# An eleven-stage kernel on one core: head projections in f32, expert chunks of 1024 tokens, and splits a batch ahead

## The reference

```python
h = _L0_tok_ref(x, ...)                       # ((gamma * (q @ k.T)) @ v) @ Wo + bo, PReLU
h = concatenate([h, txt], axis=1)
h = h + _L0_attn_ref(_layernorm(h), ...)      # 8 heads of 8, relative bias, softmax; out @ proj_w + proj_b
h = h + _L0_ffn_ref(_layernorm(h), ...)       # 16 experts, top 2, relu
h = h + _L1_attn_ref(_layernorm(h), ...)      # linear attention, D_inv = 1/max(q.k_sum, 1e-6); out @ Wproj.T + bproj
h = h + _L1_ffn_ref(_layernorm(h), ...)       # causal attention with 4 heads of 16, x + y @ wo.T, then 8 experts with
                                              # hidden 170, top 2, silu(x @ w1.T) * (x @ w3.T) @ w2.T
```

## Time and profile before

| | us |
|---|---|
| median of three runs | 2953.19 (2952.58 to 2969.43) |
| the profiled execution | 2956.11, its span 2954.3 |
| TensorE busy | 2502.1 (85%), granted clock 0.897 of full |
| VectorE, ScalarE, GpSimd busy | 2019.2, 1629.4, 400.4 |
| `mix`, from the span's start | 0 to 284 |
| `prj` | 1347 to 1415 |
| `lpr` | 1912 to 1974 |
| `cpj` | 2482 to 2569 |
| second expert stage | 2569 to the end |

### The profile page before, as it was taken

How to read it: one execution, slowest core, us unless ns; L and a number is a source line. 1 busy time by engine, 2 the same in 40 slices (tenths; PEclk the granted TensorE clock), 3 DMA queues, 4 the chain that set the end, 5 groups by cost and what they waited for, 6 DMA issues and landing times. The chain is left out here.

```text
span 2954.3 us, 54673 instructions
## 1 busy us (share of the span) xinstructions
PE 2502.1 (85%) x19289; PEld 1131.7 (38%) x19336; DVE 2019.2 (68%) x5195; ACT 1629.4 (55%) x2762; POOL 400.4 (14%) x521
## 2 busy tenths in 40 slices
PE   5887658999999999995599997856599996499999
PEld 3232642333333333334233333545444443333333
DVE  5566667888888888873477775657576773366665
ACT  2331663777777777775344444646556765344443
POOL 0002110000000000004112111051101011211110
PEclk9999776999999999997799997855599998589999
DMA  2000892122122112205300101234522221500010
GB/s 72 22 15 19 240 290 68 52 55 55 37 55 55 55 38 55 56 8 113 62 17 17 25 13 31 58 94 135 176 78 68 69 63 49 128 20 22 23 30 14
DMA packets 308961, 188.47 MB, mean 64 GB/s; under 512 B 262530, under 2 KB 263875, under 8 KB 307443
## 3 DMA queue, kind: packets, MB, share of 16 engines
q1 hardware_dynamic: 298330, 165.91, 20.7%
q0 software_dynamic: 10368, 19.06, 2.1%
HBM read 103.27 MB, written 81.69 MB: 63 GB/s over the span
## 5 line engine op out<-in xcount | busy, mean ns | idle before, releaser
L1586 DVE TENSOR_REDUCE att_mpart<-ps 128x1 f32<-128x512 f32 x1024 | 637.1, 684 | 80.6 <-PE ps L1395 47.9
L1543 ACT ACTIVATE att_p<-ps 128x704 f32<-128x704 f32 x768 | 543.1, 760 | 138.9 <-PE ps L1459 133.8
L1488 PE MATMUL ps<-att_p,att_v 128*32 128x352 f32 x3072 | 308.0, 472 | 0.1
L1395 PE MATMUL ps<-att_kT,att_qT 64*128 64x512 bf16 x1024 | 274.4, 387 | 27.2 <-DMA att_qz<-qt_d 13.9
L1459 PE MATMUL ps<-att_qm,att_kT 64*128 64x352 bf16 x1536 | 251.2, 317 | 10.7 <-ACT att_p L1543 7.8
L1220 DVE TENSOR_REDUCE cau_mpart<-ps 128x1 f32<-128x512 f32 (+5 forms) x384 | 193.3, 552 | 89.8 <-PE ps L1046 77.2
L2317 ACT ACTIVATE mo_act<-ps,mo_b 128x768 f32<-128x768 f32 x176 | 156.3, 901 | 129.7 <-PE ps L2199 128.0
L2510 DVE TENSOR_TENSOR mo_g<-mo_act,ps 128x768 f32<-128x768 f32 x176 | 167.4, 951 | 78.9 <-PE ps L2234 43.0
L1187 ACT ACTIVATE cau_p<-ps 128x704 f32<-128x704 f32 (+6 forms) x272 | 171.5, 660 | 81.7 <-PE ps L1105 49.6
L2886 ACT ACTIVATE mo_act<-ps 128x768 f32<-128x768 f32 x132 | 107.1, 811 | 196.1 <-PE ps L2801 196.0
L1459 PEld LDWEIGHTS ps<-att_qm,att_kT 64*128 64x128 bf16 x1536 | 82.4, 93 | 279.5 <-issue 263.2
(11 more groups left out here) (490 smaller groups left out, 4541.6 us busy)
## 6 DMA issues: line engine op xcount, KB each, us to landing
v_d<-pre_v SPq DMA_DIRECT2D x32, 288.0 KB, 4.2
qs_d<-pre_qs SPq DMA_DIRECT2D x8, 1152.0 KB, 6.3
att_qs<-qs_d SPq DMA_DIRECT2D x32, 288.0 KB, 4.6
att_v<-v_d SPq DMA_DIRECT2D x32, 288.0 KB, 4.5
qt_d<-pre_qT SPq DMA_DIRECT2D x8, 1056.0 KB, 4.6
kt_d<-pre_kT SPq DMA_DIRECT2D x8, 1056.0 KB, 7.5
att_kT<-kt_d SPq DMA_DIRECT2D x32, 264.0 KB, 2.8
att_qT<-qt_d SPq DMA_DIRECT2D x32, 264.0 KB, 3.2
```

Source lines behind the costliest of these rows:

```text
L1395: mm = pe.matmul(ps[:, bank, :], qT[half(s), u, j * P:(j + 1) * P], kT[half(s), u, c * BANK:(c + 1) * BANK], start=True, stop=not near)
L1488: mm = pe.matmul(ps[32 * cg:32 * cg + 32, 7, 0:TH], v[:, u, i, s, :], p[:, r, s, :], start=i < 2, stop=i == FULL - 1)
L1543: e = act.activation(p[:, n % PRING, :, :], ps[:, bank:bank + 2, 0:TH], ACT.Exp)
L1586: red = dve.tensor_reduce(mpart[:, j, s, c:c + 1], ps[:, bank, :], AX.X, ALU.max)
```

## The change

Four parts. (1) In `mix` gamma is loaded before the rows of batch 1, its transposes come in another order, and ScalarE's split stands apart from `front` and runs a batch earlier. (2) The two attention stages and the linear attention call `ahead` at the end of SP's list, so `fetch` of the projection that follows runs there; each stage's `ready` is kept in a table so that it can be used before the stage is entered. (3) `project` is written anew. (4) `expert_units` takes chunks of 1024 tokens: eight, and a last one of 256.

```diff
@@ token_mix, SP
             load(0, 0)
+            for i in range(nt):
+                sp.dma_start(gam[:, i, :], a["L0_tok_d_gamma_batched"][i * P:(i + 1) * P, :]).then_inc(gam_in[i // 4], 16)
             load(1, 1)
...
@@ token_mix, PE: gamma's transposes by GT = (*range(0, NS, 2), *range(1, NS, 2))
@@ token_mix, ACT
-            def front(b, par):
+            def split(b, par):
                 arrived(act, x_in, b, par)
                 at_least(act, S["xt_mm"], b * 2)
...
                 act.activation(xs[:, :, 1, :], xrest[:, :, :], ACT.Identity).then_inc(S["mid_made"], 1)
+
+            def front(b, par):
                 at_least(act, S["v_mm"], b)
...
                     front(b + 1, 1 - par)
+                if b + 2 < B:
+                    split(b + 2, par)
+
+            split(0, 0)
             act.wait_ge(S["wv_mm"], 1)
...
             front(0, 0)
+            split(1, 1)
@@ attend_heads, attend_causal, linear_attn: the end of SP's list
+            ahead(sp, const)
@@ project: buffers
-        xs = nm.sb("xs", [P, 2, NT, 4, C], BF16)
-        x1 = nm.sb("x1", [P, NPAD], BF16)
-        x2 = nm.sb("x2", [P, NPAD], BF16)
...
+        osum = nm.sb("osum", [HR, 2, N]) if NO == 2 else None
+        den = nm.sb("den", [P, 2, NT, heads])
+        rden = nm.sb("rden", [P, 2, NT, heads])
+        att = nm.sb("att", [P, 2, NT, C])
+        xT = nm.sb("xT", [P, 2, N])
+        w = nm.sb("w", [P, C])
         res = nm.sb("res", [P, 2, NT, C])
+        hn = nm.sb("hn", [P, 2, NT, C])
@@ project, SP
+        parts = ((0, C), (C, HR))
+        def load(sp, b, par):
+            arrived_heads(sp, b)
+            if NO == 2:
+                at_least(sp, S["sum_made"], b - 1)
+            else:
+                at_least(sp, S["ot_mm"], b - 1)
+            for r0, r1 in parts:
+                sp.dma_start(o[r0:r1, par, :, :], o_d[bass.ds(b, 1), :, r0:r1, :].rearrange("b e r n -> r (b e) n"))\
+                    .then_inc(o_in[par], 16)
...
         def fetch(sp):
+            load(sp, 0, 0)
+            sp.dma_start(w[0:C, :], w_in_d).then_inc(S["w_in"], 16)
             if bias_d is not None:
+                sp.dma_start(w[C:KW, :], bias_d.rearrange("(o c) -> o c", o=1)).then_inc(S["w_in"], 16)
+            load_rows(sp, 0, 0)
+            load(sp, 1, 1)
+            load_rows(sp, 1, 1)
...
+            load(sp, 2, 0)
+            for b in range(B):
+                if b + 3 < B:
+                    load(sp, b + 3, (b + 1) % 2)
                 if b == B - 1:
                     ahead(sp, const)
+                store(b, b % 2)
                 if b + 2 < B:
+                    load_rows(sp, b + 2, b % 2)
@@ project, POOL
+            if bias_d is not None:
+                pool.memset(xT[C:KW, :, :], 1.0).then_inc(S["one_set"], 1)
...
+                pool.tensor_tensor(osum[:, par, :], o[:, par, 0, :], o[:, par, 1, :], ALU.add).then_inc(S["sum_made"], 1)
...
+            pool.wait_ge(S["ot_mm"], B)
@@ project, PE
+            def turn(b, par):
+                at_least(pe, S["xt_cp"], b * 3)
+                for t in range(NT):
...
+                    mm = pe.transpose(ps[0:C, XT + t // 4, (t % 4) * P:(t % 4) * P + rows(t)], att[0:rows(t), par, t, :],
+                                      const["eye"][0:rows(t), 0:rows(t)])
...
             def back(b, par):
...
+                    mm = pe.matmul(ps[0:rows(t), bank, col:col + C], xT[0:KW, par, t * P:t * P + rows(t)], w[0:KW, :],
+                                   start=True, stop=True)
...
             front(0, 0)
+            for b in range(B):
+                turn(b, b % 2)
+                if b + 1 < B:
+                    front(b + 1, (b + 1) % 2)
+                if b > 0:
+                    back(b - 1, (b - 1) % 2)
             back(B - 1, (B - 1) % 2)
@@ project, ACT
+            for b in range(B):
+                par = b % 2
+                at_least(act, S["y_mm"], (b - 1) * 2)
+                for c in range(3):
+                    n = min(4 * P, N - 4 * c * P)
+                    act.wait_ge(S["xt_mm"], b * 3 + c + 1)
+                    act.activation(xT[0:C, par, 4 * c * P:4 * c * P + n], ps[0:C, XT + c, 0:n], ACT.Identity).then_inc(S["xt_cp"], 1)
@@ project, DVE: front(b + 1), then back(b - 1)
+                dve.tensor_tensor(hn[:, par, 0:FULL, :], ps[:, Y, :].rearrange("p (t c) -> p t c", c=C), res[:, par, 0:FULL, :],
                                   ALU.add).then_inc(S["hn_made"], 1)
...
@@ expert_units
+    MT, EN = 8, BANK
+    MK = -(-B * N // (2 * EN))
     N_UNITS = MK * UN
+    def en(j):
+        return min(EN, (B * N - j * 2 * EN) // 2)
+    def mt(j):
+        return 2 * en(j) // P
...
-                    mm = pe.matmul(ps[:, Z1[n % 2] + s, 0:EN], w13[halves(s), 0, column(n):column(n) + P],
-                                   x1[halves(s), j % 2, :], start=True, stop=True)
+                    mm = pe.matmul(ps[:, Z1[n % 2] + s, 0:en(j)], w13[halves(s), 0, column(n):column(n) + P],
+                                   x1[halves(s), j % 2, 0:en(j)], start=True, stop=True)
```

More of the change, by code:

```diff
@@ L969, in body, with ready @@
             step(IT - 1, True)
+        arrived_heads = const["ready_of"][const["building"] - 1]
+        def ready(sp, b):
+            for x in stored:
+                sp.wait_ge(x, 32 * PPB * (b + 1))
+        const["ready_of"][const["building"]] = ready
         yield None
-        arrived_heads = const["ready"]
         @block.sync
@@ L1779, in back @@
             def back(b, par):
-                pe.wait_ge(S["xt_cp"], b * 3 + 3)
                 at_least(pe, S["hn_made"], b * 2)
                 for t in range(NT):
-                    for i, (x, w) in enumerate(((x1, wA), (x1, wB), (x2, wC))):
-                        mm = pe.matmul(ps[:, 5 + t // 8, (t % 8) * C:(t % 8 + 1) * C], x[:, t * P:(t + 1) * P], w[:, :],
-                                       start=i == 0, stop=i == 2)
-                mm.then_inc(S["y_mm"], 1)
-            def step(b, par, first, last):
-                if not first:
-                    stacks(b - 1, 1 - par)
-                if not last:
-                    front(b + 1, 1 - par)
-                if not first:
-                    back(b - 1, 1 - par)
@@ L1879, in back @@
-                at_least(dve, S["stored"], b * 32)
-                dve.tensor_tensor(hn[:, 0:FULL, :], ps[:, 5, :].rearrange("p (t c) -> p t c", c=C), more[:, 0:FULL, :],
-                                  ALU.add).then_inc(S["hn_made"], 1)
-                dve.tensor_tensor(hn[0:TT, FULL, :], ps[0:TT, 6, 0:C], more[0:TT, FULL, :], ALU.add).then_inc(S["hn_made"], 1)
-            def step(b, par, first, last):
-                if not last:
-                    add_parts(b + 1, 1 - par)
-                    front(b + 1, 1 - par)
-                if not first:
-                    back(b - 1, 1 - par)
@@ new lines, in back @@
+                dve.wait_ge(S["y_mm"], b * 2 + 1)
+                dve.tensor_tensor(hn[:, par, 0:FULL, :], ps[:, Y, :].rearrange("p (t c) -> p t c", c=C), res[:, par, 0:FULL, :],
+                                  ALU.add).then_inc(S["hn_made"], 1)
+                dve.wait_ge(S["y_mm"], b * 2 + 2)
+                dve.tensor_tensor(hn[0:TT, par, FULL, :], ps[0:TT, Y + 1, 0:C], res[0:TT, par, FULL, :], ALU.add)\
+                    .then_inc(S["hn_made"], 1)
+            front(0, 0)
+            for b in range(B):
+                if b + 1 < B:
+                    front(b + 1, (b + 1) % 2)
+                if b > 0:
+                    back(b - 1, (b - 1) % 2)
@@ L3067, in load, with step @@
                 sp.dma_start(h[0:TT, par, FULL, :], h_b[bi, TX:N, :].rearrange("b n c -> (b n) c")).then_inc(h_sem[par], 16)
-            def step(b, par, ahead):
-                if ahead:
+            def step(b, par, more):
+                if more:
                     sp.wait_ge(S["xn_made"], (b + 1) * NT)
@@ L3759, in program @@
             const["no"] = no
-            const["ready"] = next(stages[no])
+            next(stages[no])
             if no > 1:
```

416 lines of the change are left out of this document (162 added, 254 removed).

## The result

The changed kernel takes 2935.66 us in the median of eight runs (2918.89 to 2948.74), the kernel before 2957.84 in eight (2946.30 to 2969.43): a ratio of 0.992, 95% interval 0.9898 to 0.9943. I had forecast 2870, a gain of 83; the gain is real and about a quarter of that.

| to | before | after | change | forecast |
|---|---|---|---|---|
| first load of `pre` (end of `mix`) | 285.7 | 272.3 | −13.4 | −18.1 |
| last store of `att` | 1063.1 | 1064.0 | +0.9 | 0 |
| last `hn` of `prj` | 65.1 | 70.6 | +5.5 | −10.5 |
| first `xn` of `lin` | 403.4 | 403.0 | −0.4 | +1.4 |
| last store of `lin` | 94.8 | 100.4 | +5.6 | 0 |

A forecast was written before the change was run, and what follows sets the result against it. TensorE bounds the experts, a chain over engines the projections, late splits delay the first stage. First stage −18.1, projections −9.1, −14.8, −32.1, experts −9.4 sum to −83.5: 2956.1 to 2872.6, forecast 2870, range 2845 to 2905 us.

The forecast's parts named there:

- The pace: Projections: time per batch 5.4, 4.7 and 5.2 us, set by transfers, in the second by TensorE with some half clock.
- P: Projections: the period per batch between `hn` adds, taken as 5.4, 4.7 and 5.2 us.
- The first rival: Projections: TensorE stays at half clock, P = 7.6, first batch 16.5; whole −35, 2918 us; chance 0.11.
- first batch: Projections: first transpose to first `hn`, 16.5 us at half clock, 11.0 at full, taken 15.6.
- The fill: Projections' start: loads issued a stage early leave only GpSimd's work; first transposes at 1353.9, 1914.8, 2486.3 (were 1357.6, 1918.5, 2495.9).
- The split of the load: Third projection: `o`'s 68 rows loaded as 64 and 4 go over more queues; transfers take 5.1 us a batch.
- the rival of narrow loads: Third projection: loads stay narrow, P = 7.9, 16 us later; whole −67, 2886 us; chance 0.07.
- The last store: Projections' end: store behind SP's fetch 2.1, 1.5, 2.1 us late at full clock, none at half; taken 1.4, 1.0, 1.4.
- First stage: `mix`: split a batch ahead saves 4.77 us at six boundaries, less 1.96 each, plus 1.2 at the start: −18.
- The hold: First stage: GpSimd's two subtractions stretch VectorE's copies, costing 2 × 0.98 us a step.
- Experts: Expert stages: chunks of 1024 tokens take 40.9 us each; with fill +2.3 and tail −0.9, −9.4 us.

The follow-up runs named there:

- e2: Changed kernel plus eight unread 512-column bf16 matmuls after the first front and each turn of the projections; median 2918.1 us.
- e5: e2 with each load of `o` in the projections issued one store earlier on SP; median 2902.7 us.
- e10: Changed kernel without the three calls of `ahead`; median 2918.9 us in two runs.
- e3: Changed kernel with `o` loaded by one DMA again instead of in two parts; median 2932.0 us.
- e11: e7 with GpSimd's clearings held until VectorE has made the first stage's last stacks and last but one activation; median 2856.0 us, ratio 0.9638 to the kernel before.
- e7: Changed kernel with e4's late split, early loads of `o`, and six unread bf16 matmuls a batch in projections and linear attention; median 2869.0 us.
- e4: Changed kernel with each first-stage split held back until VectorE has made the stacks of the batch before; median 2927.7 us.

## Why the prediction was wrong

- **The pace, the step that failed.** "I take P = 5.4 (transfers), 4.7 (TensorE with some half clock) and 5.2." It was 7.33, 6.57 and 7.40 with the short gaps at the end counted, and 7.06 or more without. The clock stayed at 0.50 with the pieces given (e2), and behind it stood the order of SP's list (e5), which was in no term and no rival. The transfers, which set P in the first and third projection, were not the bound, neither here nor in e5. The first rival had P = 7.6 and +5.0, +6.8 (its +3.9 counts the −2.9 behind the stage too) and −16.8 for the stages; measured +5.5, +2.5 and −16.1. Its mechanism was the right one, but that two of its numbers come so near is in part luck: its first batch was too long (16.5 for 14.3, 14.8 and 13.9 measured), and it had no wait for SP's list. I gave it 0.11, with the argument that the experts, which keep TensorE busy, have 1.00. But their matmuls have 384 columns. The rows that I had of small f32 pieces were mostly at half clock, and the earlier trace rows showed 0.65 in a stage whose bf16 pieces the change was about to take out.
- **The fill** was right in size: the first transpose in `prj` 6.5 us after GpSimd's first issue, 1.85 and 2.4 for the row of ones and the sum (forecast 1.9, 2.6). Its cause was the wait for the clearings, not `ahead` (e10). The first batch took 14.3 from first transpose to `hn` (1355.6 − 1341.3) at half clock, which the prediction priced at 16.5; its 15.6 came nearer only because it counted on some full clock.
- **The split of the load** was right: the rival of narrow loads did not come, and e3 shows what it would have cost.
- **The last store** behind SP's fetch came without delay, as the prediction said for half clock: 1407.72, right after the last add.
- **First stage.** That a split a batch ahead saves 4.77 a step was right: 31.25 to 26.45 where nothing is held (e11). The hold was right in kind and too large in size, 1.3 a step in place of 2 × 0.98, so a step gained 3.5 and not 2.8. The first end copy came 0.8 later (79.51 for 78.75) where the prediction had 1.2 earlier; why is open. Missing was what GpSimd does with the time it gains: the clearings for the next stage lengthened their step by 7.7 us in the changed kernel (35.43 for 27.72) and by 14.2 in e5's profile.
- **Experts.** Right: the adds that end a chunk answer to the earlier trace rows and stand 40.92 apart, forecast 40.9, and the part gave −9.9 for −8.0.

```profile
2649.59 0.69 DVE L2967 TENSOR_TENSOR mo_res<-ps,mo_hx 128x512 f32<-128x512 f32 x1
...
2690.51 0.69 DVE L2967 TENSOR_TENSOR mo_res<-ps,mo_hx 128x512 f32<-128x512 f32 x1
```

- **The stages between** (`att`, `lin`, `cau`), whose work the change leaves as it was, added 8.5 (+0.9, +5.6, +2.0). The linear attention alone can differ by 23 us between profiles, so the range should have had some 10 us for it.

## What to carry to other kernels

Price a TensorE stage at both clock levels, and ask for the level not how busy the engine will be but which of the present stages is made of the same pieces; a stage of small f32 transposes and products may stay at half clock with TensorE full, and a few long bf16 matmuls that nobody reads can shorten it. When an engine is relieved, look at what stands next in its list: here GpSimd's clearings for the next stage moved into VectorE's copies. Compare stages rather than wholes, and see in several profiles how far a stage of unchanged code moves, before a gain of a few microseconds is credited. And before crediting an earlier issue, find which wait holds the queue now; in one list, the place of a load behind a store can be the bound.

## What the runs showed of the hardware

- TensorE busy 8.00 of 8 us with f32 transposes and 64-column products kept a granted clock of 0.50; with eight 512-column bf16 matmuls a batch among them, and no larger share of busy time (56.59 of 66 us for 57.22), it read 0.81 to 0.91.
- One stage with the same instructions took 87.7 to 110.7 us, by its clock (0.91 to 0.62).
- A VectorE operation of 0.49 us took 11.79 (e7) or 4.03 (e4) beside the same three back-to-back clearings on GpSimd of 3.94, and a copy of 0.28 took 12.41 (e5).
- A load of 68 rows in one DMA gave a batch every 8.51 us, in 64 and 4 rows 7.40.
